# A graph layer's gather loop: four sums of an iteration in one PSUM bank, one-hots two iterations ahead, 24 slots for gathered rows

## The reference

```python
src = node_feature[edge_src]
parts = [relu(node_feature)]
for t in range(3):
    msg = relu(src @ W_e[t].T + b_e[t])
    msg = where((edge_type == t)[:, None], msg, 0)
    parts.append(segment_sum(msg, edge_dst, num_segments=N))
agg = concatenate(parts, axis=1)
for t in range(3):
    o = agg @ W_n[t].T + b_n[t]
    updated = where((node_type == t)[:, None], o, updated)
x = layernorm(x + updated + node_feature)
```

## Time and profile before

| | |
|---|---|
| median of 3 runs | 1012.33 us (1012.32 to 1013.22) |
| the profiled execution | 1012.83 us, its span 1010.9 us |
| GpSimd busy | 756.2 us (75%), 808 instructions |
| TensorE busy | 700.0 us (69%), mean granted clock 0.748 of full |
| VectorE busy | 512.2 us (51%) |
| ScalarE busy | 132.3 us (13%) |
| first gather of the loop starts, last one starts | 99.81 us, 998.11 us |

### The profile page before, as it was taken

How to read it: one execution, slowest core, us unless ns; L and a number is a source line. 1 busy time by engine, 2 the same in 40 slices (tenths; PEclk the granted TensorE clock), 3 DMA queues, 4 the chain that set the end, 5 groups by cost and what they waited for, 6 DMA issues and landing times.

```text
span 1010.9 us, 9119 instructions
## 1 busy us (share of the span) xinstructions
PE 700.0 (69%) x2671; PEld 459.3 (45%) x2671; DVE 512.2 (51%) x1187; ACT 132.3 (13%) x350; POOL 756.2 (75%) x808
## 2 busy tenths in 40 slices
PE   6761477776767767776767687667876676768576
PEld 4430354454444544544444455444544454445344
DVE  6999544454445444544544454445444542443433
ACT  3581001000100100010001001000100010121010
POOL 7777777777777777777777777777777777777774
PEclk9895557777876877677778767786677776797869
DMA  7774323222222222222222222212223232222221
GB/s 222 237 272 90 55 54 82 53 78 81 53 78 79 53 80 60 71 78 55 79 79 52 80 67 64 78 53 81 78 53 91 80 91 78 61 69 79 62 66 40
DMA packets 52653, 83.75 MB, mean 83 GB/s; under 512 B 15059, under 2 KB 34688, under 8 KB 52606
## 3 DMA queue, kind: packets, MB, share of 16 engines
q0 software_dynamic: 25312, 51.89, 19.9%
q1 hardware_dynamic: 24734, 27.41, 8.5%
q10 hardware_dynamic: 2560, 3.88, 1.3%
HBM read 70.32 MB, written 12.80 MB: 82 GB/s over the span
## 4 chain that ended last, share of the span: by engine, by line
POOL 65%; issue 22%; DVE 5%; DMA 4%; PE 2%; SPq 0%; ACT 0%; POOLq 0%; DVEq 0%
POOL tab L510 63%; DMA tab<-message_table,idx_t 3%; POOL xg L506 2%; PE ps L1219 2%; DVE tab L870 2%; DMA dst_raw<-in_dst 1%; DVE src_raw L760 1%; DVE dst_raw L758 0%; DVE first_f L736 0%; DVE h L1000 0%; PE ps L1260 0%; SPq L335 0%; ACT acc L585 0%; POOLq L122 0%; DVE loop_f L732 0%
## 5 line engine op out<-in xcount | busy, mean ns | idle before, releaser
L510 POOL DMA_INDIRECT tab<-message_table,idx_t x720 | 680.1, 945 | 219.4 <-issue 216.1
L1219 PE MATMUL ps<-work,tab 128*128 128x126 f32 x1440 | 272.1, 349 | 273.7 <-DMA tab<-message_table,idx_t 273.4
L1219 PEld LDWEIGHTS ps<-work,tab 128*128 128x128 f32 x1440 | 241.4, 252 | 370.4 <-issue 361.8
L923 DVE TENSOR_TENSOR work<-key_t,ps 128x504 f32<-128x504 f32 x180 | 122.0, 679 | 419.0 <-PE ps L1219 417.0
L1260 PE MATMUL ps<-wn_t,stage 128*128 128x384 f32 x294 | 150.2, 637 | 1.4 <-DVE stage L1027 1.4
L506 POOL DMA_INDIRECT xg<-in_x,esrc_t x68 | 71.0, 1043 | 21.6 <-issue 18.9
L1260 PEld LDWEIGHTS ps<-wn_t,stage 128*128 128x128 f32 x294 | 69.0, 265 | 29.6 <-issue 23.0
L931 DVE TENSOR_TENSOR acc<-ps,acc 128x126 f32 x216 | 61.3, 284 | 24.4 <-PE ps L1219 13.2
L1252 PE MATMUL ps<-wn_t,stage 128*128 128x384 f32 x98 | 73.2, 846 | 0.0
L1251 PE MATMUL ps<-bn_row,ones 1*128 1x384 f32 x98 | 69.5, 803 | 1.2 <-DVE mv L1005 0.9
L626 ACT ACTIVATE xst<-ps 128x256 f32<-128x256 f32 (+1 forms) x36 | 13.7, 381 | 416.2 <-PE ps L1193 416.2
(11 more groups left out here) (167 smaller groups left out, 486.8 us busy)
## 6 DMA issues: line engine op xcount, KB each, us to landing
tab<-message_table,idx_t POOLq DMA_INDIRECT x720, 2.5
message_table<-tab SPq DMA_DIRECT2D x24, 384.0 KB, 3.4
wn_raw<-message_table SPq DMA_DIRECT2D x22, 384.0 KB, 3.4
xg<-in_x SPq DMA_DIRECT2D x11, 256.0 KB, 4.0
work<-in_x ACTq DMA_DIRECT2D x10, 256.0 KB, 4.1
out<-xg SPq DMA_DIRECT2D x10, 256.0 KB, 3.4
xg<-in_x,esrc_t POOLq DMA_INDIRECT x68
wn_raw<-in_L_gnn_W_n ACTq DMA_DIRECT2D x1, 768.0 KB, 9.9
```

The lines of the kernel that those rows point to most:

```text
L510: pool.indirect_dma_start(msg[:, slot, :], None, table, bass.IndirectOffsetOnAxis(ap=rows, axis=0)).then_inc(signal, 16)
L923: dve.tensor_tensor(hot[:, n * g:n * g + n, :], keys.broadcast_to((P, n, T * WIN)), iota_ps.rearrange("p (o c) -> p o c", o=1).broadcast_t ...
L1219: ins = pe.matmul(sums_bank(nth), msg[:, GC * g + c, :], hot[:, GC * g + c, :], start=(c == 0), stop=(c == GC - 1))
```

## The change

- The four sums of an iteration go into four column ranges of one bank, iterations in turn into banks 0 and 1 (`SUM_PS`, `sums_at`). TensorE waits for the additions of the iteration two before, not of three sums before. VectorE adds all four at the end of an iteration. The last iteration is an exception: its sums go to four places and are added one by one.
- The one-hots are made two iterations ahead, in two buffers (`hots`), of which the second lies where the setup kept `src_raw` and `first_f`. Those of iterations 0 and 1 are made before the loop.
- The gathered rows have 24 slots (`RING` = 6 groups of four) instead of 16. A group waits for the sum of the group six before.
- The stages of early chunks and of node tiles lie at other places of the iteration: the early sum two iterations after its turning, in bank 2 beside the turned chunk (`early_place`); tile j-1 is turned and its self rows are placed after group 2 of iteration j; the whole linear layer of tile j-2 comes after group 1; `finish_acc` of tile j-1 comes at the end of iteration j on VectorE, `finish_y` of tile j-3 after group 0.

On TensorE, the last iteration before: the sums are L1219, tile 42's types L1260 with `stage0` (the first two behind group 0, the third behind group 1), tile 43's turning L1242 ahead of group 2, and tile 44 uses `stage1`.

The diff, cut to its core (of the removed lines of the two `iteration` functions on VectorE and TensorE most are left out, they stand above; left out too: names and waits of the early chunks' setup, SyncE's waits, which name `e_placed` for `e_turned`, and a branch that isn't taken with these inputs):

```diff
 NG, GC = 4, 4
+RING = 6
...
 
-AGG = (0, 1, 2)
+SUM_PS = (0, 1)
 LIN_PS, FIN_XT_PS = (3, 6), (5, 7)
-E_XT_PS, E_MSG_PS = 5, (6, 7)
+E_PS, E_MSG_PS = 2, (6, 7)
+E_SUM_AT, TURN_AT = 2 * P, T * P
 SETUP_BANKS, LATE_BANKS = (0, 5), (2, 3)
 PEELED = 4
 MSG_PS, XT_PS = 1, (6, 7)
...
-        def sums_bank(nth):
-            return ps[:, AGG[nth % len(AGG)], 0:T * WIN]
+        def sums_at(j, g):
+
+            if j < NI - 1:
+                bank, col = SUM_PS[j % 2], g * T * WIN
+            else:
+                bank, col = (SUM_PS[j % 2], E_PS, SUM_PS[1 - j % 2], SUM_PS[j % 2])[g], 0
+            return ps[:, bank, col:col + T * WIN]
+
+        early_at = ps[:, E_PS, E_SUM_AT:E_SUM_AT + T * WIN]
+
+        def free_before(j, g):
+
+            if j < NI - 1:
+                return sums_ahead(j - 2, NG) if j > 1 else 0
+            return (sums_ahead(j - 2, NG), ALL_SUMS - NG * 2, sums_ahead(j - 1, NG), sums_ahead(j, 1))[g]
...
                 for g in range(NG):
-                    if j > 0:
-                        pool.wait_ge(group_summed, NG * (j - 1) + g + 1)
-                    for slot in range(GC * g, GC * g + GC):
-                        gather(slot, idx_t[:, 2 * j + slot // HC, slot % HC:slot % HC + 1], gathered[g])
+                    n = NG * j + g
+                    if n >= RING:
+                        pool.wait_ge(group_summed, n - RING + 1)
+                    for c in range(GC * g, GC * g + GC):
+                        gather(n % RING * GC + c % GC, idx_t[:, 2 * j + c // HC, c % HC:c % HC + 1],
+                               gathered[n % RING])
 
             pool.wait_ge(ctl_set, 1)
             need = pool.value_load(ctl[0:1, 0:1], min_val=0, max_val=1)
...
-            def finish_x(nth, z=0, first=False):
+            def finish_x(nth, z=0, first=False, placed=True):
                 act.wait_ge(fin_xt[z], nth + 1)
+                if z == 0 and placed:
+                    act.wait_ge(self_placed[0], nth + 1)
                 if not first:
                     act.wait_ge(fin_lin[z], nth)
-                act.activation(stage[z][:, 0, :], ps[:, FIN_XT_PS[z], 0:P], ACT.Relu).then_inc(stage_xt[z], 1)
+                at_col = turn_at(z)
+                act.activation(stage[z][:, 0, :], ps[:, FIN_XT_PS[z], at_col:at_col + P], ACT.Relu
+                               ).then_inc(stage_xt[z], 1)
...
+                if fin:
+                    mask_selfs(j - 1)
                 if early:
                     early_copy(j)
+                if last:
+                    finish_sd(j - 2)
                 if fin:
-                    mask_selfs(j - 1)
-                    finish_x(j - 1, first=isinstance(j, int) and j == 1)
-                if j > 1:
-                    finish_sd(j - 2)
+                    finish_x(j - 1, first=j == 1)
                 if extra is not None:
                     finish_sd(extra, 1)
                 if last:
                     finish_sd(j - 1)
                     finish_sd(KE, 1)
+                elif j > 1:
+                    finish_sd(j - 2)
...
-                dve.tensor_tensor(hot[:, n * g:n * g + n, :], keys.broadcast_to((P, n, T * WIN)),
+                dve.tensor_tensor(hots[j % 2][:, n * g:n * g + n, :], keys.broadcast_to((P, n, T * WIN)),
                                   iota_ps.rearrange("p (o c) -> p o c", o=1).broadcast_to((P, n, T * WIN)),
                                   ALU.is_equal).then_inc(hot_ready, 1)
...
-            def add_sums(nth, base):
+            def add_sums(nth, sums, base):
 
                 cols = acc[:, :, bass.ds(base, WIN)]
                 dve.wait_ge(added, nth)
-                dve.tensor_tensor(cols, sums_bank(nth).rearrange("p (t c) -> p t c", t=T), cols, ALU.add
-                                  ).then_inc(added, 1)
+                dve.tensor_tensor(cols, sums.rearrange("p (t c) -> p t c", t=T), cols, ALU.add).then_inc(added, 1)
...
-                if j > 1:
-                    finish_acc(j - 2, j - 2, 0, sums_ahead(j))
+            def iteration(j, extra=None):
+                last = j == NI - 1
+                bases_of = load_bases(j, 1 < j <= NE + 1)
+
+                def add_group(g):
+                    add_sums(sums_ahead(j, g), sums_at(j, g), bases_of[g])
+
                 for g in range(NG):
                     dve.wait_ge(group_summed, NG * j + g + 1)
...
+                    if j + 2 < NI:
+                        one_hot(j + 2, g)
+                    if g == 0 and j > 2:
+                        finish_y(j - 3, j - 3)
+                    if g == 1:
+                        if j > 1:
+                            dve.wait_ge(stage_acc[0], j - 1)
+                        if 1 < j <= NE + 1:
+                            early_add(j - 2, bases_of[NG])
+                        if extra is not None:
+                            finish_acc(ORDER[extra], extra, 1, sums_ahead(j))
+                    if g == FIN and 0 < j <= NE:
+                        early_hot(j - 1)
+                        early_select(j - 1)
+                    if last:
+                        if g == FIN + 1:
+                            dve.wait_ge(stage_acc[0], j)
+                        add_group(g)
+                        if g == 1:
+                            finish_h(j - 2, j - 2)
+                        if g == FIN:
+                            finish_acc(j - 1, j - 1, 0, sums_ahead(j, g) + 1)
+                            finish_y(j - 2, j - 2)
+                if last:
                     finish_acc(ORDER[KE], KE, 1, ALL_SUMS)
+                    dve.wait_ge(fin_y[0], j - 1)
+                    finish(j - 1, j - 1)
+                    finish(ORDER[KE], KE, 1)
+                    return
+                if extra is not None:
+                    dve.wait_ge(stage_acc[1], extra + 1)
+                for g in range(NG):
+                    add_group(g)
+                if j > 0:
+                    finish_acc(j - 1, j - 1, 0, sums_ahead(j, NG))
+                if j > 1:
+                    finish_h(j - 2, j - 2)
                 if extra is not None:
                     finish(ORDER[extra], extra, 1)
...
...
-            for g in range(NG):
-                one_hot(0, g)
+            for j in range(2):
+                for g in range(NG):
+                    one_hot(j, g)
...
                 pe.wait_ge(self_masked[z], nth + 1)
-                pe.wait_ge(stage_xt[z], nth + 1)
+                if z == 1:
+                    pe.wait_ge(stage_xt[z], nth + 1)
                 part = self_rows(tile, z)
                 n = part.shape[0]
...
...
+            def iteration(j, extra=None, loads=None):
+                last = j == NI - 1
                 for g in range(NG):
...
+                    n = NG * j + g
+                    if free_before(j, g):
+                        pe.wait_ge(added, free_before(j, g))
+                    pe.wait_ge(hot_ready, n + 1)
                     if last and g == FIN + 1:
                         linear_types(NA - 1, 0)
...
+                    pe.wait_ge(gathered[n % RING], GC * 16 * (n // RING + 1))
+                    sum_group(j, g, n % RING)
+                    if g == 0:
+                        if 0 < j <= NE:
+                            early_make(j - 1)
+                        if j <= NE + 1:
+                            early_place(j)
+                        if extra is not None:
+                            finish_turn(ORDER[extra], extra, 2, 1, extra == 0)
+                        if last:
                             finish_turn(ORDER[KE], KE, 2, 1)
                             linear_open(KE, 1)
                             place_selfs(ORDER[KE], KE, 1)
...
                     if g == 1:
...
+                        if j > 1:
+                            finish_linear(j - 2, first=j == 2)
                         if extra is not None:
                             linear_open(extra, 1, extra == 0)
                             place_selfs(ORDER[extra], extra, 1)
                     if g == FIN:
...
+                        if j > 0:
+                            finish_turn(j - 1, j - 1, loads, first=j == 1)
+                            place_selfs(j - 1, j - 1)
                         if extra is not None:
                             linear_types(extra, 1)
...
+                        if last:
+                            linear_open(j - 1)
```

199 lines of the change are left out of this document (68 added, 131 removed).

## The result

| | before | changed |
|---|---|---|
| median of 6 runs each | 1012.87 us (1012.32 to 1013.22) | 1016.96 us (1014.46 to 1018.05) |
| the profiled execution, its span | 1012.83, 1010.9 us | 1017.05, 1015.1 us |
| last gather starts, behind it to the span's end | 998.11, 12.8 us | 997.90, 17.2 us |
| last sum starts, behind it to the span's end | 1000.62, 10.3 us | 1005.26, 9.8 us |
| mean granted clock, TensorE busy | 0.748, 700.0 us | 0.751, 658.3 us |

The ratio is 1.0034 (95% interval 1.0024 to 1.0044): slower by 4.1 us.

A forecast was written before the change was run, and what follows sets the result against it. GpSimd, issuing gathers without waiting for 898 of 1010.9 us, was taken as the bound. Head and loop 0, last iteration +3.65, end -0.45 give +3.2 us on 1012.33: 1015.5 us, own range 1014.3 to 1016.6, whole 1013.0 to 1018.2.

The forecast's parts named there:

- Loop at nothing: Head and gather loop: slots, one-hots, bank and moved additions cost 0 us; first gather near 99.81, last near 998.11.
- The serial chain: Last iteration: tile 42's products, VectorE, root, tile 43's ReLU and products precede the last sum; +3.65 us.
- X: End of tile 42's products in the last iteration, forecast at 998.3; the last sum starts 6.0 us later.
- -0.45 us at the end: After the last addition: tile 42's last two VectorE steps move ahead, saving 0.45 us.
- the whole range: Time over all cases: 1013.0 us (inside the high-clock case) to 1018.2 us (most of the late case).
- the rival with a chance of 0.19: Last iteration: TensorE's clock rises late or falls again; +5 to +6 us, about 1017.8; chance 0.19.
- the forecast with 0.52: Tail: clock low from about 986 to near 995; +3.2 us, 1015.5 us, own range 1014.3 to 1016.6.
- Clock high: Last iteration: clock stays high or rises by 991 to 992; +0.35 to +1.9 us, about 1013.4; chance 0.22.
- A late rise: Last iteration: a clock rise at 998 gives +5 to +6 us, about 1017.8; within the case of chance 0.19.
- both rivals about it: GpSimd's loop step shrinks (about 1011 us, chance 0.04) or grows (3 ns a step, 1017.7 us, chance 0.03).
- all-low bound of +9: Tail wholly at the low clock: X at 1001.0, last sum at 1010.2, net +9 us; chance 0.03.

The follow-up runs named there:

- e12: Changed kernel with tile 44's early stages in iteration 42, tile 42's linear layer and tile 43's turning behind group 0, VectorE steps earlier; chip 9: 1012.11 against 1012.33 us.
- e10: Kernel before with only the changed order of the last iteration on TensorE, and tile 42's root ahead of tile 43's ReLU; chip 0: 1017.49 against 1012.42 us.
- e11: Changed kernel plus five unused 128x384 products on TensorE behind the last sum of iteration 43; chip 9: 1014.65 us against 1012.33 for the kernel before.
- e5: The same kernel as e10, the kernel before with only the last iteration's order changed, on chip 8: 1174.84 against 1173.88 us, ratio 1.0011.
- e8: The same kernel as e12, the changed kernel with the last iteration's chain taken apart, on chip 8: 1181.61 us against 1173.88 for the kernel before, ratio 1.0072.

## Why the prediction was right, step by step

- **Loop at nothing: right.** First gather at 99.67 (forecast 99.81 within 0.3), last at 997.90 (998.11 within 1). e12, with the tail repaired, is no slower than the kernel before. (One reading behind it was off: a gather lands in at most 4.7 us in the trace of before, not 4.07, so the slack was about 9.5 us and not 10; nothing hangs on the difference.)
- **The serial chain: right in every link.** The last sum is released by tile 43's types, the root stands ahead of the ReLU. From the end X of tile 42's products to the last sum the forecast was 6.0 us; it is 1005.26 - 999.35 = 5.9. e10 and e12 show from both sides that this order is the loss.
- **X was 1.05 us too early: the mis-sized term.** Forecast 998.3, measured 999.35. The clock fell at 984.3, not "from about 986", and stayed low for 13.7 us, not 9. Up to group 1's sum this hardly mattered (TensorE went on at 993.53; forecast 994.1), but then bias, x and part of the types ran low: 993.53 to 999.35 is 5.8 us where 3.52 + 0.45 + 0.2 was assumed. The low stretch of 976.2 to 989.9 in the earlier trace rows, 13.7 us, would have been the better guess; I took a length between two that had been seen.
- **-0.45 us at the end: right.** From the last sum to the end of the span 9.8 us (forecast 9.8, before 10.3).
- The sum was +3.2, the measured +4.1 us: X's 1.05 us less 0.1 in the chain is the difference. The time itself, 1016.96, is 1.5 us above 1015.5, because the prediction also counted from 1012.33, the median of three runs, where six runs gave 1012.87.
- **Inside the whole range, above the forecast's own.** 1016.96 lies just outside 1014.3 to 1016.6, on the side of the late clock. The chain was forecast well, but as to the clock it is the rival with a chance of 0.19 that came true, not the forecast with 0.52.
- **The rivals.** Clock high: not in the profiled execution of this kernel, but e11 brought it about for most of the chain, and its first group of runs, 1012.3 to 1013.5, lies around this rival's 1013.4 or under it. Its price at the end, +0.35 us for a wholly high clock, stands against 0.8 us in e11's trace, where 3.4 us were still low. Two of the changed kernel's six runs (1014.46, 1014.86) stand apart from the rest, without a trace. A late rise (at 998, +5 to +6) is what happened in the clock, with +4.2 in time: its price was a microsecond too high, as tile 43's products ran wholly at the high clock (0.91 and 2.10 us at 1001.74 and 1003.32). GpSimd's step kept its length, so both rivals about it fall.
- The rule that a TensorE that waits for DMA drops back to the low clock and starts the next burst cold (the Trainium skill, "TensorE: Matmul & The Clock Gate", section "HAM oscillation — how this bites in real kernels") is borne out at 985.41, where the sum takes 2.05 us behind 3.84 us of waiting, and by e11, where with that wait filled it takes 1.13. Taken for every burst, as in the prediction's all-low bound of +9, it goes too far: tile 43's burst at 1001.74 stands behind a wait of 1.06 us, for ScalarE and not for DMA, and ran at the high level (0.91 us).

## What to carry to other kernels

Where one engine issues without waiting for 898 of 1011 us, a rearrangement of the others that never makes it wait is felt ahead of its first instruction and behind its last: price the tail first, link by link, and ask of each moved stage whether its result is now needed by an engine that was already ahead. A burst of matmuls behind a wait may run at the lower clock; keep such a burst off the last chain, or give it work earlier, rather than count on the clock. Where a kernel's runs fall in two groups, as e11's 12 do, 2.3 us apart, a median of few runs can be a microsecond or two off; that the changed kernel's wider spread comes from the clock is likely and not shown, as the kernel before also spread over 2 to 4 us in its longer series.

## What the runs showed of the hardware

- The same kernel took 1012 us on chips 0 and 9 and 1170 to 1174 us on chips 8 and 11, with gathers of the same 0.94 us, and the order of two kernels turned round between them: e10's edit costs 5.1 us and e12's nothing on chips 0 and 9, e5's 1.0 and e8's 7.7 us on chip 8.
- With five products that nobody needs (3.39 us of TensorE's time) half of the changed kernel's runs were faster than any of its eleven without them (1012.29 to 1013.51 against 1014.46 and more); in the one that was traced the low-clock stretch was 3.4 us instead of 13.7.
- Two executions with nearly the same order in the last iteration (e10's and the changed kernel's) had the clock rise at 992.6, ahead of tile 42's products, and at 998, within them. They differ by 2.0 us in all, and the last sum stands 1.5 us closer to the last gather in the first.
